# A two-layer kernel (attention with experts, then a state-space filter with a linear gate): the last attention group rearranged, output division moved later, third maximum scores moved ahead of a filler

## The chip, the cores and the metric

The kernel is one program on one NeuronCore of a Trainium2 chip. The metric is the device time of one execution in microseconds (us), lower is better; the figure shown is the median of three executions. PE is the matrix engine (TensorE), DVE the vector engine, ACT the scalar engine, POOL is GpSimd, SP the engine that only issues transfers here.

## What is computed

The input x is 4 sequences of 512 tokens with 512 values. Cut to what matters:

```python
xn = layernorm(x)
q, k, v = rope(xn @ wq), rope(xn @ wk), xn @ wv      # 32 heads of 16, 8 key/value heads
s = softmax(causal(q k^T / 4)) v @ wo
y = relu(xn @ W_e[top 2 of 8 experts] + b_e)          # mean of the two
x = x + s * silu(y.mean)
xn = layernorm(x)
K = s4_taps(Lambda, p, q, Vc, Ct, B, step)            # 512 real taps, by Cauchy sums and an inverse DFT
s = causal_convolution(xn, K) + D * xn
g = silu(xn @ dequant(weight).T + bias)
out = x + s * g
```

## The kernel before

The program has three parts, and each engine has its own list of instructions for each of them.

**Part a** (`sp_a`, `dve_a`, `pool_a`, `act_a`, `pe_a`) takes the 16 tiles of 128 tokens one after the other: layer norm, transposition, the products with wq, wk, wv and the gate, each value split in a high and a low part, rotation, and the ranking of experts. At its end the tokens are sorted into 39 expert tiles. While the vector engine makes the sorting tables, PE runs dummy products (`keep_awake`, L948), then `pe_back`, which needs those tables.

**Part b** (`dve_b`, `act_b`, `pool_b`, `sp_b`, `pe_b`) runs over 4 sequences b and 8 key/value heads h: 32 groups (b, h). A group of four query heads has ten *maximum scores* (`scores_1`, n = 0 to 9, L1563), whose row maxima DVE takes straight from the PSUM bank (`maxima`, L1374; three banks in turn, so scores n wait for maxima n - 3). DVE then writes the negated maxima as two parts (`maxima_parts`, L1387 and L1389), PE turns them (`turn_maxima`, L1600), DVE copies them (`maxima_rows`, L1397), and SP and ACT store them behind the group's queries (`maximum_rows`, L1291, semaphore b_mr). Ten *second scores* (`scores_2`, L1589 and L1592), the first of which waits for b_mr, contain the maximum; ACT takes exp (L1486), POOL clears the masked halves of four diagonal blocks (`select`, L1308), and PE multiplies with the values (`values`, L1616) into bank 4. DVE turns that bank (`rows_of`, L1407), divides by the row sums (`normalise`, L1412 and L1416) and, after every second group, turns the pair (`pair_rows`, L1424) for the output projection.

Three groups are in flight on PE: while second scores of (b, h) run, so do maximum scores of the next group, and 0 and 1 of the group after. Between them stand *fillers* (`quarters`, gaps 0 to 4): quarters of an expert tile (L1642, L1644) or of an output projection (`project`, L1655), six or eight in most groups, one or two in gap 4. DVE also turns gathered expert rows (`expert_x`, L1438) and makes the Cauchy sums of the filter in six steps for each of four pieces, one step in a group (`dve_s4`, L652 on); after the last piece it computes 512 complex roots in one go (L703 to L737), in group (3, 6). The inverse DFT (`pe_taps`, L762) is eight full-width products with broadcast weights in group (3, 7); the taps go to DRAM and come back as a Toeplitz tile (`sp_taps`).

**Part c** (`*_c`) is the second layer on 16 tiles: gather of expert outputs (`rows`, `more_rows` on POOL), gate, layer norm, then on PE a turn (L2061), the linear product (L2072) and the convolution (L2077). Before its first tile stand the last sequence's output projection (16 products, `project` in `pe_c`) and the scaling and splitting of the linear weights on DVE (`dve_scale`, L1878, L1884, L1887). `prepared(u)` on DVE (L1895 to L1917) makes the gated sum and statistics of tile u; `inverse_root` on POOL (L1850) needs them, and `shift`, the norm on ACT (L2026) and PE's turn follow.

The order of part b on PE, in the body of the loop over groups:

```python
scores(e, (2, 3, 4), following, (0, 1, 2), (b, h))
quarters(b, h, 0)
...
scores(e, (0, 1), after, (8, 9), (b, h))
quarters(b, h, 3)
for j in ORDER[1:]:
    values(e, b, h, j)
quarters(b, h, 4)
```

## Time and profile before

| | |
|---|---|
| median of 3 executions | 697.06 us (695.39 to 698.77) |
| the profiled execution | 695.48 us |
| its span, first to last instruction | 693.3 us |
| busy: PE, DVE, POOL, ACT | 92%, 80%, 51%, 42% |
| granted PE clock, mean | 0.97 |
| stretches: part a, part b, part c from its first linear product | 0 to about 104 us, to about 593 us, 607 us to the end |

The profiled execution is 2.2 us longer than its span and 1.6 us under the median. In a timeline row the first number is the start from the span's begin, the second the duration; what stands in brackets is the time its engine stood idle before it and what ended that. A group of rows by line gives busy time, mean duration in ns, and the idle time before. PE "busy" is modelled from the issue of its products. A granted clock of 1.00 is 2.4 GHz, 0.50 is 1.2 GHz.

### The profile page before, as it was taken

The numbers are of one execution on the slowest core, as the hardware profiler recorded it, in microseconds if no ns is written. First come the engines' busy times: TensorE is split into PE (matmuls) and PEld (weight loads), VectorE is DVE, ScalarE is ACT, GpSimd is POOL, SyncE is SP. The second block draws the span as 40 slices with busy tenths as digits, with TensorE's granted clock in tenths as the row PEclk, the third lists the DMA queues.
The fourth block names the chain that finished last, engine by engine and source line by source line (L and its number), as shares of the span: only waits on it lengthen the run. The fifth ranks groups of instructions, "written<-read, shape, count | busy, mean of one in ns | idle before, by whom it ended". The sixth has DMA issues, their size and how long they took to land.

```text
span 693.3 us, 12356 instructions
## 1 busy us (share of the span) xinstructions
PE 638.2 (92%) x3560; PEld 344.0 (50%) x3560; DVE 553.4 (80%) x1789; ACT 289.0 (42%) x535; POOL 351.1 (51%) x497
## 2 busy tenths in 40 slices
PE   8999997888989999989999898999998999999997
PEld 4888774433333334333443333443333443488886
DVE  5698898669987777987777798787887887769995
ACT  4353326234443444434454443444344543445441
POOL 3777531636764723466473245646415434566630
PEclk9999999569999999999999999999999999999999
DMA  7599989246667454272653606457063526758851
GB/s 251 151 330 281 331 195 180 50 68 179 106 191 125 98 96 75 40 134 77 114 96 64 92 22 131 106 99 128 20 117 64 142 80 215 152 119 220 201 132 76
DMA packets 55567, 92.67 MB, mean 134 GB/s; under 512 B 10328, under 2 KB 23320, under 8 KB 55504
## 3 DMA queue, kind: packets, MB, share of 16 engines
q1 hardware_dynamic: 41890, 66.45, 41.0%
q0 software_dynamic: 8576, 18.62, 12.7%
q10 hardware_dynamic: 5038, 6.84, 3.9%
q8 instruction: 29, 0.48, 0.3%
q14 instruction: 34, 0.28, 0.2%
HBM read 61.93 MB, written 29.43 MB: 132 GB/s over the span
## 4 chain that ended last, share of the span: by engine, by line
PE 46%; DVE 39%; issue 6%; DMA 3%; POOL 3%; SPq 1%; ACT 1%; ACTq 0%; DVEq 0%; POOLq 0%
DVE bank L1374 19%; PE bank L1644 10%; PE bank L1616 7%; PE bank L1563 6%; PE bank L2072 6%; DVE arena L1374 4%; PE bank L2077 4%; PE bank L991 4%; DMA turned_parts<-qk_parts 3%; DVE arena L1407 2%; PE bank L1655 2%; DVE m_parts L1387 2%; PE bank L1589 2%; PE bank L1600 2%; DVE arena L1424 2%
## 5 line engine op out<-in xcount | busy, mean ns | idle before, releaser
L1374 DVE CUSTOM_DVE_ANT_0 bank<-bank,cst 128x384 f32<-128x384 f32 (+3 forms) x512 | 234.0, 522 | 66.8 <-PE bank L1563 65.2
L1486 ACT ACTIVATE arena<-bank 128x512 f32<-128x512 f32 x320 | 172.7, 600 | 209.6 <-PE bank L1589 149.9
L1321 POOL DMA_INDIRECT arena<-xn_rows,slots_i x156 | 150.1, 962 | 55.0 <-issue 37.3
L1308 POOL TENSOR_SCALAR_AFFINE_SELECT arena<-arena 128x512 f32<-128x512 f32 x128 | 81.0, 647 | 182.9 <-ACT arena L1486 181.8
L1644 PE MATMUL bank<-w_e,arena 128*128 x312 | 160.4, 620 | 0.0
L1563 PE MATMUL bank<-kt,qt 48*128 48x512 f32 (+1 forms) x496 | 119.5, 352 | 15.3 <-DVE arena L1374 12.4
L1563 PEld LDWEIGHTS bank<-kt,qt 48*128 48x128 f32 x496 | 73.6, 193 | 101.6 <-DVE arena L1374 56.3
L1589 PE MATMUL bank<-qt,kt 50*128 50x512 f32 x256 | 92.2, 464 | 0.6 <-ACT arena L1486 0.6
L1616 PE MATMUL bank<-arena 128*32 128x512 f32 (+3 forms) x1024 | 88.0, 455 | 2.7 <-ACT arena L1486 2.3
L1644 PEld LDWEIGHTS bank<-w_e,arena 128*128 128x128 f32 x312 | 53.7, 192 | 57.5 <-issue 54.2
L1374 DVE DVE_READ_ACCUMULATOR2_ANT arena<- 128x1 f32 x512 | 72.0, 141 | 0.0
L1655 PE MATMUL bank<-w_proj,arena 128*128 128x512 f32 x128 | 66.9, 638 | 0.0
L991 PE MATMUL bank<-proj_high,xh 128*128 128x264 f32 (+1 forms) x128 | 45.9, 359 | 0.7 <-DVE xl L522 0.7
L825 POOL TENSOR_TENSOR s_tok<-arena 128x256 f32<-128x256 f32 (+1 forms) x64 | 33.4, 554 | 25.4 <-DVE arena L541 20.0
L1589 PEld LDWEIGHTS bank<-qt,kt 50*128 50x128 f32 x256 | 43.3, 191 | 4.3 <-ACT arena L1486 2.2
L1496 ACT ACTIVATE arena<-bank 128x512 f32<-128x512 f32 x39 | 23.4, 599 | 50.3 <-PE bank L1644 44.7
L1616 PEld LDWEIGHTS bank<-arena 128*32 128x32 f32 x1024 | 24.6, 110 | 39.3 <-issue 24.4
L991 PE MATMUL bank<-proj_low,xh 128*128 128x264 f32 (+1 forms) x128 | 43.5, 340 | 0.0
L991 PE MATMUL bank<-proj_high,xl 128*128 128x264 f32 (+1 forms) x128 | 43.2, 338 | 0.0
L1655 PEld LDWEIGHTS bank<-w_proj,arena 128*128 128x128 f32 x128 | 21.6, 193 | 27.4 <-issue 24.7
L1438 DVE STREAM_TRANSPOSE arena<-arena 128x512 f32<-128x512 f32 x39 | 27.5, 706 | 8.1 <-PE bank L1644 7.5
L537 DVE TENSOR_TENSOR arena<-bank,cst 128x128 f32<-128x128 f32 (+1 forms) x63 | 27.2, 475 | 5.9 <-PE bank L991 5.8
(168 smaller groups left out, 954.3 us busy)
## 6 DMA issues: line engine op xcount, KB each, us to landing
qt<-turned_parts SPq DMA_DIRECT2D x96, 128.0 KB
turned_parts<-qk_parts SPq DMA_DIRECT2D x8, 1280.0 KB
expert_rows<-arena SPq DMA_DIRECT2D x39, 256.0 KB
w_e<-in_L_ffn_W_e ACTq DMA_DIRECT2D x24, 256.0 KB, 6.1
kt<-turned_parts SPq DMA_DIRECT2D x96, 64.0 KB, 5.5
arena<-in_L_attn_x SPq DMA_DIRECT2D x16, 256.0 KB, 5.8
xn_rows<-arena SPq DMA_DIRECT2D x16, 256.0 KB, 5.7
w_e<-in_L_attn_x SPq DMA_DIRECT2D x16, 256.0 KB
```

Of the source, the lines that this page charges most:

```text
L825: i = g.tensor_tensor(o[:, :, :, c, :], xc[:, :, :, c, :], xs[:, :, :, 1 - c, :], op)
L991: i = t.matmul(out[u % 2][:, 0:n], x[:, u % 2, k, :], w[part][:, k, :], start=(k == 0 and x is xh and part == 0), stop=(k == KB - 1 and pa ...
L1308: g.affine_select(out=diag, in_=diag, compare_op=ALU.is_ge, fill=0.0, base=0, pattern=[[0, 2], [0, HALF], [1, P]], channel_multiplier=-1). ...
L1321: e.indirect_dma_start(xg[m % 2][:, n * P:(n + 1) * P], None, xn_q, bass.IndirectOffsetOnAxis(ap=slots_i[:, n, m:m + 1], axis=0)).then_inc ...
L1374: i = v.tensor_tensor_reduce(out=part, in0=part, in1=const("mask")[:, S - w:], scale=1.0, scalar=LOWEST, op0=ALU.add, op1=ALU.max, accum_o ...
L1486: nc.scalar.activation(pt[:, s, first:second + 1:second - first].rearrange("p c r q -> p c (r q)"), s2_bank(b, h, n).rearrange("p (c x) -> ...
L1563: i = t.matmul(s1_bank(b, h, n)[:, at:at + w], stack[rows, x if r is None else r, q * P:w], kt[rows, h // 2 % 2, h % 2, 0:w], start=(x == ...
L1589: i = t.matmul(to, keys(j), queries[:, q:q + 2], start=True, stop=True)
L1616: i = nc.tensor.matmul(bank[4][VW * r:VW * (r + 1), j * P:], vb[:, j, h, :], pt[:, r // HALF, at:at + TPB - j, r % HALF, :], start=(j == O ...
L1644: i = t.matmul(bank[7], xgt[:, m % 2, k * P:(k + 1) * P], w_e[:, ex[m], k, :], start=False, stop=(k == KB - 1))
L1655: i = t.matmul(bank[to], ot[:, (b * PAIRS + k) % (PAIRS + 1), u, :], wo[:, k, :], start=(k == 0), stop=(k == KB - 1))
L2072: i = t.matmul(bank[2 + u % 2][:, :], x[:, u % 2, k, :], (w_high, w_low)[part][:, k, :], start=(k + n == 0), stop=(k + n == KB + 1))
```

## The change

Seven edits, in the order of the program:

1. Part a, start: the second token tile is loaded behind the second of four blocks of wq, whose semaphore is split in two; statistics of tile 1 come ahead of the splitting of wq on DVE; ACT normalises tile 1 ahead of the other weights; PE turns tile 2 behind the q products of tile 1.
2. `keep_awake(16)` becomes `keep_awake(28)`.
3. The Cauchy steps run without a gap between pieces, so that the last piece ends in (3, 1), and the roots are made in four steps in groups (3, 2) to (3, 5) (`dve_roots`).
4. In a group on PE, maximum scores 2 (of the group after) and second scores 0 (of the next) stand behind the values, in front of gap 4.
5. In a group on DVE, for h > 0, the division and the turn of the pair stand behind maxima 0 and 1 of the group after, no longer between maxima 4 and 5.
6. The last group has a list of its own (`last_group`): twelve of the sixteen projection products of the last sequence stand between its scores and values, in four banks; the inverse DFT is eight 32-wide products plus one that sums the four strips; DVE divides the last group before it scales the weights, and splits the weights (`dve_scaled_parts`) after the statistics of the first tile of part c, before those of the second.
7. POOL gathers rows of tiles 1 and 2 of part c after the last select, no longer between selects. The DFT table is loaded a group earlier at its end.

The core of the diff:

```diff
@@ sp_a, dve_a, act_a, pe_a @@
-                e.dma_start(wq[:, k, :], wq_d[k * P:(k + 1) * P]).then_inc(a_wq, 16)
-            e.dma_start(xin[:, 1, :], x_t[1]).then_inc(a_x[1], 16)
+                e.dma_start(wq[:, k, :], wq_d[k * P:(k + 1) * P]).then_inc(a_wq[k // 2], 16)
+                if k == 1:
+                    e.dma_start(xin[:, 1, :], x_t[1]).then_inc(a_x[1], 16)
...
-            keep_awake(16, bank[0])
+            keep_awake(28, bank[0])
...
@@ dve_s4 @@
-            if not (isinstance(b, int) and b == NB - 1):
-                h -= 2
+            at = b * NG + h - 2
+            if at < 0:
+                return
+            piece, h = divmod(at, 6)
+            if piece == NB:
+                dve_roots(e, st, h)
...
+        def dve_tap_parts(e):
+
+            e.wait_ge(s4_parts, 1)
+            nc.vector.tensor_copy(tap_parts, bank[5]).then_inc(s4_taken, 1)
...
@@ pe_taps @@
-                e.wait_ge(b_m, NB * NG * NJ)
-            for k in range(KB):
-                i = t.matmul(bank[5], roots[:, c, k:k + 1].to_broadcast([P, P]), dft[c][:, k, :],
-                             start=(c + k == 0), stop=(c + k == KB))
+                for part in range(2):
+                    for k in range(KB):
+                        i = t.matmul(bank[5][32 * k:32 * (k + 1), :], roots[:, part, k:k + 1].to_broadcast([P, 32]), dft[part][:, k, :],
+                                     start=(part == 0), stop=(part == 1), skip_group_check=True)
+                i.then_inc(s4_parts, 1)
             if c == 1:
-                i.then_inc(s4_taps, 1)
+                e.wait_ge(s4_taken, 1)
+                t.matmul(bank[5], const("sel")[:, 0:1].to_broadcast([P, P]), tap_parts, start=True, stop=True).then_inc(s4_taps, 1)
...
@@ dve_b @@
-                    finish(*next_group(b, h, -1))
+                    done, later = next_group(b, h, -1), h > 0 and following
+                    rows_of(*done)
+                    if not later:
+                        divided(*done)
...
+                    if later:
+                        divided(*done)
                     if (b, h) == (NB - 1, NG - 1):
+                        dve_tap_parts(e)
+                        dve_taps(e, st)
+                        finish(b, h)
                         dve_scale(e)
-                        dve_taps(e, st)
                     dve_s4(e, st, b, h)
-                    if following is None:
-                        finish(b, h)
...
@@ pe_b @@
-                    scores(e, (2, 3, 4), following, (0, 1, 2), (b, h))
+                    scores(e, (3, 4), following, (1, 2), (b, h))
...
+                    scores(e, (2,), after, (0,), following)
                     quarters(b, h, 4)
+
+            def last_group(b, h):
...
+                e.wait_ge(b_m, NB * NG * NJ)
+                fill(0, 2)
+                scores(e, (), None, (1, 2), (b, h))
+                fill(2, 3)
+                scores(e, (), None, (3, 4), (b, h))
+                pe_taps(e, 0)
+                scores(e, (), None, (5, 6, 7), (b, h))
+                values(e, b, h, ORDER[0])
+                fill(3, 4)
+                scores(e, (), None, (8, 9), (b, h))
+                pe_taps(e, 1)
+                fill(4, 5)
+                values(e, b, h, ORDER[1])
+                fill(5, 6)
+                values(e, b, h, ORDER[2])
+                fill(6, 7)
+                values(e, b, h, ORDER[3])
+                fill(7, 12)
...
@@ dve_c @@
             e.wait_ge(b_s, TPB)
-            for u in range(2):
-                prepared(u)
+            prepared(0)
+            dve_scaled_parts(e)
             shift(0, 0)
+            prepared(1)
...
@@ pe_c @@
             for u in range(TPB):
-                if u > 1:
-                    e.wait_ge(b_s, (NB - 1) * TPB + u - 1)
-                if u == TPB - 1:
-                    turn(0, 0)
-                for k in range(KB):
-                    project(NB - 1, u, k, 7 - u % 2)
+                project(NB - 1, u, KB - 1, PROJECT_BANK[u])
+            e.wait_ge(b_s, (NB - 1) * TPB + 2)
+            turn(0, 0)
```

What moves, first on PE in group (3, 4) to (3, 5). L1616 (L1658 in the changed file) are values, L1563 (L1605) maximum scores, L1589 (L1631) second scores, L1644 (L1686) a filler. Before:

```order
L1616 MATMUL bank4<-arena 32x256 x4
L1616 MATMUL bank4<-arena 32x128 x4
L1616 MATMUL bank4<-arena 32x384 x4
L1644 ISA
L1644 MATMUL bank67<-w_e,arena 128x512
L1563 MATMUL bank5<-kt,qt_56 128x512
L1589 MATMUL bank67<-qt_56,kt 128x512
L1563 MATMUL bank0<-kt,qt_56 128x512
L1589 MATMUL bank2<-qt_56,kt 128x512
```

And in the changed kernel:

```order
L1658 MATMUL bank4<-arena 32x256 x4
L1658 MATMUL bank4<-arena 32x128 x4
L1658 MATMUL bank4<-arena 32x384 x4
L1605 MATMUL bank5<-kt,qt_56 128x512
L1631 MATMUL bank67<-qt_56,kt 128x512
L1686 ISA
L1686 MATMUL bank67<-w_e,arena 128x512
L1605 MATMUL bank0<-kt,qt_56 128x512
L1631 MATMUL bank2<-qt_56,kt 128x512
```

The pair of scores stands a filler earlier; nothing else changes places there.

DVE at the entry of part c: bank 4 is turned and divided for the last group (L1407 to L1424, in the changed file L1440 to L1457), the linear weights are scaled and split (L1878 to L1887; L1953 to L1966), and `prepared(0)` begins with a product into s_tok (L1895; L1974). Before:

```order
L1878 TENSOR_TENSOR w_e<-w_e,arena 128x512 x4
L1884 CAST w_high_60<-w_e 128x512 x4
L1887 TENSOR_TENSOR w_low_61<-w_e,w_high_60 128x512 x4
L744 MEMSET arena 128x128
L745 COPY arena<-bank5 128x512
L747 TENSOR_TENSOR arena<-arena,d_c 128x1
L1407 STREAM_TRANSPOSE arena<-bank4 128x512
L1412 RECIPROCAL arena<-arena 128x16
L1416 TENSOR_TENSOR arena<-arena 128x16x16
L1424 STREAM_TRANSPOSE arena<-arena 128x512
L1895 TENSOR_TENSOR s_tok<-s_tok,w_e 128x512
```

And in the changed kernel:

```order
L1440 STREAM_TRANSPOSE arena<-bank4 128x512
L1445 RECIPROCAL arena<-arena 128x16
L1449 TENSOR_TENSOR arena<-arena 128x16x16
L1457 STREAM_TRANSPOSE arena<-arena 128x512
L1953 TENSOR_TENSOR w_e<-w_e,arena 128x512 x4
L1974 TENSOR_TENSOR s_tok<-s_tok,w_e 128x512
L1980 TENSOR_TENSOR s_tok<-s_tok,w_e 128x512
L1985 BN_STATS arena<-s_tok 128x6
L1991 BN_AGGR arena<-arena 128x2
L1996 TENSOR_SCALAR arena<-arena 128x1
L1963 CAST w_high_60<-w_e 128x512 x4
L1966 TENSOR_TENSOR w_low_61<-w_e,w_high_60 128x512 x4
```

The weight work that stood ahead of the last division now stands behind it, and its split behind the first `prepared`.

## Rows read from the trace of the kernel before

**Rows 1.** The stretch of the groups, 150 to 573 us, busy us of PE, PEld, DVE, ACT, POOL.

```profile
150.00:573.00 423.00, 389.73 (x2206) 162.63 (x2204) 339.27 (x1251) 180.57 (x338) 214.60 (x265) 0.99 0.51 100
```

**Rows 2.** The same stretch: who waited, for whom (us in total, times, longest).

```profile
PE bank L1600 <- DVE m_parts L1389: 12.8, 24, 1.0
...
DVE bank L1374 <- PE bank L1563: 59.6, 34, 5.3
```

**Rows 3.** The same stretch, PE groups by form (busy, mean ns, idle before).

```profile
L1563 PE MATMUL bank<-kt,qt 48*128 48x256 f32 x116 | 26.8, 323 | 12.9 <-DVE arena L1374 10.1 <-issue 2.7
```

**Rows 4.** PE timeline, one period (start us, us, what).

```profile
501.33 0.28 PE L1600 MATMUL bank<-cst,m_parts 128*32 128x128 f32 x1 [0.86 <-DVE m_parts L1389]
...
504.69 1.98 PE L1644 MATMUL bank<-w_e,arena 128*128 x4
...
515.87 0.28 PE L1600 MATMUL bank<-cst,m_parts 128*32 128x128 f32 x1 [0.27 <-DVE m_parts L1389]
```

**Rows 5.** DVE timeline, the same period.

```profile
507.24 0.70 DVE L1374 CUSTOM_DVE_ANT_0 bank<-bank,cst 128x512 f32<-128x512 f32 x1 [1.95 <-PE bank L1563]
...
510.02 0.25 DVE L1412 RECIPROCAL arena<-arena 128x16 f32<-128x16 f32 x1
510.31 0.42 DVE L1416 TENSOR_TENSOR arena<-arena 128x256 f32<-128x256 f32 x1
510.76 0.71 DVE L1424 STREAM_TRANSPOSE arena<-arena 128x512 f32<-128x512 f32 x1
```

**Rows 6.** The store of turned maxima: ACT queue timeline, then PE weight loads.

```profile
501.96 0.62 ACTq L1291 DMA_DIRECT2D qt<-arena  x1
...
573.81 0.62 ACTq L1291 DMA_DIRECT2D qt<-arena  x1
...
576.45 0.29 PEld L1589 LDWEIGHTS bank<-qt,kt 50*128 50x128 f32 x3 [0.62 <-DMA qt<-arena]
```

**Rows 7.** PE timeline around the dummy products, then 116 to 148 us (us, busy, clock, DMA).

```profile
108.56 3.63 PE L948 MATMUL bank<-ones_b 128*128 128x512 bf16 x16
115.25 1.97 PE L1156 MATMUL bank<-arena 128*128 128x78 bf16 x32 [3.06 <-DVE arena L1089]
...
116.00:148.00 32.00, 25.92 (x159) 0.55 0.31 55
```

**Rows 8.** PE groups by form, last group and projections, 573 to 607 us.

```profile
L1655 PE MATMUL bank<-w_proj,arena 128*128 128x512 f32 x32 | 14.2, 595 | 0.0
L762 PE MATMUL bank<-v_tok,roots 128*128 128x512 f32 x8 | 5.4, 840 | 0.4 <-DVEq L737 0.4
L762 PE MATMUL bank<-s_tok,roots 128*128 128x512 f32 x8 | 3.7, 605 | 0.0
...
L1616 PE MATMUL bank<-arena 128*32 128x512 f32 x8 | 1.1, 604 | 0.0
```

**Rows 9.** DVE groups, 584 to 595 us, then its timeline.

```profile
L1887 DVE TENSOR_TENSOR w_low<-w_e,w_high 128x512 fp32r<-128x512 f32 x4 | 2.5, 684 | 0.0
L1878 DVE TENSOR_TENSOR w_e<-w_e,arena 128x512 f32<-128x512 f32 x4 | 2.5, 686 | 2.9 <-DMA arena<-n_L_ffn_weight_scale_inv 2.9
L1884 DVE CAST w_high<-w_e 128x512 fp32r<-128x512 f32 x4 | 2.3, 634 | 0.0
...
592.54 0.72 DVE L1407 STREAM_TRANSPOSE arena<-bank 128x512 f32<-128x512 f32 x1
...
594.68 0.65 DVE L1895 TENSOR_TENSOR s_tok<-s_tok,w_e 128x512 f32<-128x512 f32 x1
...
597.31 0.68 DVE L1895 TENSOR_TENSOR s_tok<-s_tok,w_e 128x512 f32<-128x512 f32 x1
```

**Rows 10.** Entry of the second layer: POOL timeline, then PE timeline.

```profile
608.26 0.57 POOL L1850 TENSOR_TENSOR arena<-arena,cst 128x1 f32<-128x1 f32 x1 [3.57 <-DVE arena L1917]
...
618.27 0.66 PE L2061 MATMUL bank<-cst,w_e 128*128 128x128 f32 x4 [1.25 <-ACT w_e L2026]
```

**Rows 11.** PE timeline at the start of the program.

```profile
22.57 0.66 PE L961 MATMUL bank<-cst,arena 128*128 128x128 f32 x4 [0.96 <-ACT arena L858]
```

More of the change, by code:

```diff
@@ L975, in sequence @@
                         e.wait_ge(a_xl[u % 2], nth(b, u))
-                    if (u + 1 < TPB or more) and (b, u) != (0, 0):
+                    early = b == 0 and u < 2
+                    if (u + 1 < TPB or more) and not early:
                         turn(b + (u + 1) // TPB, (u + 1) % TPB)
@@ L2042, in act_c @@
             gate(e, 0, 2)
-            projected(e, NB - 1, 3, 6)
             gate(e, 0, 3)
```

135 lines of the change are left out of this document (81 added, 54 removed).

## The prediction

> **What bounds the kernel now.** I read the busy time by stretch first. The groups fill 423 us of the 693, and PE is busy for 389.7 of them, DVE for 339.3 [rows 1]: PE is the bound, with 33 us of gaps, and the reader should ask who makes the gaps. The waits answer: PE stood 12.8 us in 24 places before the turn of the maxima, for DVE [rows 2], and 12.9 us before the last maximum scores (n = 8 and 9), nearly all for DVE too [rows 3]. Together that is 25.7 us, and it is odd, for DVE itself stood 59.6 us waiting for PE's maximum scores [rows 2]. So neither is full; they wait for each other in turn. The timelines of one period show how. PE turned maxima at 501.33, 0.86 late; its values ended at 504.69, and then came two products of filler in front of the third maximum scores [rows 4]. DVE had run dry 1.95 us before it could start on those scores at 507.24; later, between its fifth and sixth maxima, it spent 510.02 to 511.47 on the division and the turn of the pair [rows 5], at a time when PE was about to ask for maxima, and the next turn of maxima came 0.27 late [rows 4].
>
> **The steady groups.** The edit on PE puts the third scores at about 504.7 instead of 506.6, so DVE can take them up to 1.9 us sooner; the edit on DVE moves 1.45 us (in every second group the 0.25 and 0.42 alone, 0.7) to before them, into the time in which it stood idle [rows 5]. In this period, then, the sixth maxima begin when their scores are there, 1.7 us earlier than before, and the turn, late by 0.27, would have over a microsecond in hand. The arithmetic of PE does not change, so the gain can be no more than its waits for DVE: 25.7 us [rows 2, 3]. Not all of it comes back. Three times in the program `expert_x` on DVE stands behind the expert of gap 4, so that DVE still starts late; the Cauchy steps and expert turns fill most of the idle time into which the division goes; and where maxima end just behind a select on POOL DVE's small operations are long already. I take 70%, 18 us. From below I bound it at 9 (about a third: the waits before scores 8 and 9 go by two thirds, those at the turn stay), from above at 25.7.
>
> What the moved pair of scores is late for next is a transfer. Second scores 0 wait for the store of the turned maxima. That store is issued 0.63 us behind the turn (501.96 against 501.33) and in the one place where PE came early, at 573.81, its landing was over by 576.45, 2.64 us later [rows 6]; that makes 3.27 behind the turn. In the new order PE wants it 3.4 to 3.6 us behind the turn (504.69 - 501.33 = 3.36, and the product of third scores) [rows 4]. I cost this at nothing, covered by 0.1 to 0.3 us; without the cover each 0.1 us costs 3 us over 30 groups.
>
> The Trainium skill, "DMA: Bandwidth & Descriptors", section "Issuing engines are not separate DMA queues", says that transfers of all issuing engines run on the same 16 DMA engines and interleave, so that issuing on ACT and SP buys no private path. By that rule the store lands later when stacks and gathers are in flight. The trace neither confirms nor denies it for this store: PE never came early enough elsewhere.
>
> **Start of the program.** The loads and statistics of tile 1 move ahead, and DVE's statistics of tile 2, on which POOL's memsets and the norm of tile 3 hang, come some 0.7 us sooner (one statistics pass no longer stands in between). PE waited 0.96 us for that norm and is then full [rows 11]. Between 0 and -0.9; part of it is lost where part a later waits for transfers, so -0.4.
>
> **Dummy products.** Sixteen took 3.63 us, twelve more take 2.7 and fill most of the 3.06 us in which PE waited [rows 7]: they end about 0.3 us before the tables are there. What they buy is the clock: behind that wait its mean from 116 to 148 us was 0.55, nearly all at the 1.2 GHz level [rows 7]. About 3 us of products at full clock instead of half give 1.2 us (half of the 1.97 us of `pe_back` and a little behind it). Bounds: +0.3 if they end late, -8 if the clock then stays up until 148 us (PE is busy for 25.92 us there, about half of which a full clock would save, and I let a third of that be covered by waits for others), which I doubt, since PE stands idle again, 6 of the 32 us, and the half clock outlasted those 25.92 us of products [rows 7]. The Trainium skill, "TensorE: Matmul & The Clock Gate", Part 1, has idleness bring the half clock back; by it the later pause undoes the gain behind it, and the term is the 1.2 us taken here.
>
> **The last group and the entry of the second layer.** Let T be the last turn of maxima, 573.81 - 0.63 = 573.18 [rows 6]. The last values ended at 592.5, T + 19.3, where DVE turns bank 4 [rows 9]. Out of PE's way go 5.4 + 3.7 us of inverse DFT and some 1.3 us of waits; in come two sets of narrow products, each like the values' four at 1.1, one full product of 0.9, and seven projections of 14.2 / 16 = 0.89 each [rows 8]: T + 19.3 - 9.1 - 1.3 + 3.1 + 6.2 = T + 18.2. PE then has nine projections left, 8.0 us, done at T + 26.2, where before it was done at T + 33.5. This is where the gain would seem to be, and I count none of it, because DVE takes over. Behind the last values it has the division (0.72, 0.25, 0.42, 0.71: 2.1), the scaling (2.5), `prepared(0)` (597.31 - 594.68 = 2.6), the split of weights (2.3 + 2.5), `prepared(1)` (2.6), the Toeplitz split and the low part of tile 0 (three passes like the 0.68 of L1887, 2.0), then `prepared(2)` (2.6) [rows 5, 9]: 19.4, so POOL can take the root of tile 2 at T + 37.6. Before, the 7.3 us of scaling and splitting lay under PE's inverse DFT, and that root began at 608.26, T + 35.1 [rows 10]. What follows it up to the third tile's products is POOL's series of gathers and roots, unchanged, which made PE stand 1.25 us at 618.27 [rows 10]. So the entry is late by 2.5 us; as overlaps of a few tenths are likely I take +2. Bounds: +4 with the clock falling while PE waits for DVE from T + 26 on, -2 if DVE's series runs beside the gathers better than one after another. The roots, for which PE waited 0.4 us [rows 8], move to groups (3, 2) to (3, 5), under PE's work, at most eight operations in each; the cover is the idle time of DVE, and without it they cost, at no more than the 0.25 us of the small reciprocal [rows 5], up to 2 us in each. From the second tile on part c is unchanged.
>
> **The sum.** -0.4 - 1.2 - 18 + 2 = -17.6, from 695.48 us of the profiled execution: 677.9. The median of the runs is 1.6 above that execution, which gives 679.5; I say 679.
>
> **Rivals.**
> *Half the gain.* DVE is the next bound: the work that a group needs from it is 339.3 / 29 = 11.7 us (the 116 products of rows 3, four a period, make 29 periods) against PE's 389.7 / 29 = 13.4, and the heavy groups lie above that mean. Then 9 us come back: 688. For it: the selects on POOL that lengthen its small operations, and that every idle microsecond into which the division goes may be wanted. Against: in the period of rows 5 it fits. 0.17.
> *The clock stays up after the dummy products*, and the early groups run at full clock: 8 us instead of 1.2, 672. Against it the pauses behind them. 0.09.
> *Nothing comes of it:* the waits for DVE turn into waits for ACT to empty bank 7 and for exps, as PE arrives earlier at both: 695. The change moves only order, so this can be. 0.07.
> *Slower, by the store of the maxima.* The store lands behind the second scores' turn and each group stalls PE, the bound. Its place is the first second scores, its price 30 times (landing after issue - 2.97 us), and it cancels the 18 us when the landing takes 3.6 us. At 3.8 us it costs 25: 677.9 + 25 + 1.6 = 704. For it: that the measured case, 2.64, was a quiet moment, and the rule above. Against: it may take over a third longer before it decides. 0.05.
>
> **How the numbers follow.** The forecast's own case, 672 to 685, has 0.62. The range goes from 670, which takes in most of the clock case and of the upper bound of the group term, to 691, which takes in the half gain and its upper errors; it leaves out the last two rivals and the tails. About 0.5% (3.5 us) is what a measurement of this kernel can tell from no change. Faster: 0.62 + 0.17 + 0.09 = 0.88, less 0.01 for a half gain that turns out smaller, 0.87. Same: 0.07 and that 0.01, 0.08. Slower: 0.05.
>
> **What would show it.** Right: PE's waits before the turn of maxima and before scores 8 and 9 fall from 25.7 to under 9 us, DVE's wait for maximum scores shrinks, periods shorten from 423 / 29 = 14.6 to about 14.0 us, no wait of PE's weight loads for the store, a clock above 0.55 behind the dummy products, and 2 us more than before between the last turn of maxima and the third tile's products of the second layer. Wrong: a long total of waits for the store, periods of 14.6 us with waits under another name, or PE in the second layer starting earlier than T + 33 after the last turn.

## The result and the profile after

The changed kernel takes 691.48 us (median of 13 executions, 687.97 to 693.93), the kernel before 695.05 beside it: ratio 0.9933, interval 0.9911 to 0.9955. That is 0.7% faster where 2.5% was forecast; the direction held, the size did not, and 691.5 lies just outside the range. A second measurement on a chip like this one gave 0.9945 (0.9923 to 0.9968). Some experiments ran on chips on which the kernel before takes 683 us; there the changed kernel came to 0.9966 (0.9937 to 0.9995). So every ratio below is to the kernel before on the same chip. "First kind" is a chip of 695 to 698 us, "second kind" one of 683; several chips of each were used, and only runs that are said to be of one set were measured side by side. Executions in a slower state (up to 974 us) are left out of the ratios.

The profiled execution took 689.92 us, its span is 688.0. The stretch of the groups, who waited for whom (columns: us in total, times, longest), to be read against [rows 2]:

```profile
PE bank L1642 <- DVE m_parts L1422: 10.8, 19, 1.7
PE bank L1658 <- ACT arena L1528: 8.0, 7, 1.5
PE bank L1684 <- ACT arena L1538: 3.6, 3, 1.7
PE bank L1605 <- DVE arena L1407: 2.7, 8, 0.5
...
DVE bank L1407 <- PE bank L1605: 28.3, 42, 3.2
...
DVE bank L1407 <- remote: 15.7, 10, 2.4
```

DVE's wait for maximum scores fell from 59.6 to 28.3, or to 44.0 with the 15.7 for which the profile names no releaser ("remote"), and PE's wait for DVE before maximum scores fell from 10.1 [rows 3] to 2.7. But the wait at the turn of maxima nearly stayed, 12.8 to 10.8, and one grew that was 1.9 us before: values wait 8.0 us for ACT (4.4 in a second profile of the changed kernel, 2.0 in a second one of the kernel before).

The ledger by marks on PE, in us: end of part a (first turn of maxima) at 102.17 before, 102.42 after; from there to the next turn 29.8 and 27.7; from that to the last turn 441.2 and 433.8; behind it to the end 120.2 and 124.1. So +0.2, -2.1, -7.5, +3.9, in sum -5.4 before rounding. Forecast were -0.4, -1.2, -18 and +2. In the third stretch PE stood idle for 36.2 us before and 30.8 after, so only 5.4 us of the 7.5 are idle time that went; the other 2.1 are a balance of the clock, of the cut run and of what a wait costs beyond its idle time, each treated below.

**Why the turn still waits.** DVE, then POOL, then PE in one period after:

```profile
518.15 0.15 DVE L1407 DVE_READ_ACCUMULATOR2_ANT arena<- 128x1 f32 x1
518.33 1.40 DVE L1420 TENSOR_SCALAR m_parts<-arena 128x16 fp32r<-128x16 f32 x1
519.76 0.18 DVE L1422 SCALAR_TENSOR_TENSOR m_parts<-arena,m_parts 128x16 fp32r<-128x16 f32 x1
```

```profile
517.49 0.95 POOL L1357 DMA_INDIRECT arena<-xn_rows,slots_i  x1 [0.17 <-issue]
518.45 1.24 POOL L1344 TENSOR_SCALAR_AFFINE_SELECT arena<-arena 128x512 f32<-128x512 f32 x2
```

```profile
519.99 0.28 PE L1642 MATMUL bank<-cst,m_parts 128*32 128x128 f32 x1 [1.35 <-DVE m_parts L1422]
```

An operation on 128x16 numbers, 0.17 us elsewhere, takes 1.40 and ends at 519.73, just when POOL's two selects end (519.69). The wait is booked on DVE; POOL held it. This is not new: in the whole profile 13 first and 7 second parts took over 0.5 us, before 11 and 8, and both parts together 22 us against 24. DVE's earlier start did not take them out of the selects' way. The Trainium skill, "SBUF — State Buffer", section "Who interferes with whom", says that DVE and GpSimd share one port pair and that the later of two instructions that want it is blocked for the whole of the other. In all 20 cases a select runs beside the long part, and in 18 it is recorded as starting first, so the trace agrees; in the row shown DVE starts 0.12 us before the selects, while POOL still issues a gather.

**Why the values wait.** PE, DVE, ACT's queue and ACT, then PE again, in another period after:

```profile
548.05 0.28 PE L1642 MATMUL bank<-cst,m_parts 128*32 128x128 f32 x1
...
551.93 0.85 PE L1658 MATMUL bank<-arena 128*32 128x384 f32 x8 [1.09 <-ACT arena L1528]
```

```profile
549.76 0.28 DVE L1430 COPY arena<-bank 32x128 f32<-32x128 f32 x1 [1.14 <-PE bank L1642]
```

```profile
550.07 0.62 ACTq L1327 DMA_DIRECT2D qt<-arena  x1
550.79 1.09 ACT L1528 ACTIVATE arena<-bank 128x512 f32<-128x512 f32 x2 [3.38 <-PE bank L1658]
```

The copy of the turned maxima comes 1.71 us behind the turn (0.32 to 0.50 in most groups); ACT's store stands behind it, and the last two exps behind the store. They end at 551.88, and the values start at 551.93. From 150 us on ten groups have a copy over 0.9 us behind the turn, two in the profile before.

**What the moved pair costs PE.** From the end of the values to the filler of gap 0, PE before and after, the same work:

```profile
517.81 1.50 PE L1616 MATMUL bank<-arena 128*32 128x256 f32 x24
519.24 1.12 PE L1655 MATMUL bank<-w_proj,arena 128*128 128x512 f32 x2
520.30 0.50 PE L1563 MATMUL bank<-kt,qt 48*128 48x512 f32 x1
...
521.20 1.99 PE L1655 MATMUL bank<-w_proj,arena 128*128 128x512 f32 x4
```

```profile
508.22 1.50 PE L1658 MATMUL bank<-arena 128*32 128x256 f32 x24
509.65 0.49 PE L1605 MATMUL bank<-kt,qt 48*128 48x512 f32 x1
509.65 0.50 PE L1631 MATMUL bank<-qt,kt 50*128 50x512 f32 x1
510.08 1.13 PE L1697 MATMUL bank<-w_proj,arena 128*128 128x512 f32 x2
511.14 0.49 PE L1605 MATMUL bank<-kt,qt 48*128 48x512 f32 x1
...
511.81 1.98 PE L1697 MATMUL bank<-w_proj,arena 128*128 128x512 f32 x4
```

Without a wait in either, 519.24 to 521.20 is 1.96 us and 509.65 to 511.81 is 2.16. The other groups without a wait there say the same: 1.95 to 1.97 and 2.15 or 2.16 (once 2.23) with one quarter of filler in gap 4, 2.82 and 3.10 with two, 2.94 and 3.14 with two and the bias product that begins an expert tile. For the 15, 7 and 7 groups of these sorts that makes some 6.4 us, an estimate from these rows. With the waits, which fell a little, the stretch takes 74.6 us before and 79.7 after in 29 groups, 0.18 more a group. The six products are the same run cut in two, and cutting it costs.

**The clock** had a part as well. The stretches around one wait of PE before, and the same place after (us, busy of PE, PEld, DVE, ACT, POOL, clock, DMA):

```profile
366.00:367.00 1.00, 0.69 (x6) 0.49 (x8) 1.00 (x5) 0.37 (x1) 0.00 (x0) 1.00 0.93 109
...
368.00:371.50 3.50, 3.50 (x11) 1.11 (x7) 1.89 (x10) 0.00 (x0) 1.23 (x2) 0.54 0.21 81
```

```profile
364.00:368.00 4.00, 3.99 (x34) 1.71 (x35) 3.20 (x9) 1.09 (x2) 0.00 (x0) 1.00 0.03 8
```

Before, PE stood 1.26 and 0.26 us in front of scores 8 and 9 there, and then ran 3.5 us at the 1.2 GHz level; so again at 484 us. After it stood 0.39 and 0.26 and the clock stayed at 2.4 GHz. The two periods around the first dip took 16.07 and 14.55 us, eight groups earlier 15.70 and 13.91; those around the second 16.22 and 14.07. So a dip costs 0.7 to 1.0 us, and the two some 1.7 of the 7.5 us by which the groups got shorter in these two profiles. In other profiles of versions like the changed one, dips stand elsewhere (none to three), so this is no sure gain.

**The entry of part c.** DVE, POOL and PE behind the last turn, T = 563.86:

```profile
582.26 0.72 DVE L1440 STREAM_TRANSPOSE arena<-bank 128x512 f32<-128x512 f32 x1 [3.75 <-PE bank L1658]
...
586.77 0.69 DVE L1974 TENSOR_TENSOR s_tok<-s_tok,w_e 128x512 f32<-128x512 f32 x1
...
593.30 0.69 DVE L1974 TENSOR_TENSOR s_tok<-s_tok,w_e 128x512 f32<-128x512 f32 x1
```

```profile
602.48 0.59 POOL L1922 TENSOR_TENSOR arena<-arena,cst 128x1 f32<-128x1 f32 x1
...
610.66 1.15 POOL L1922 TENSOR_TENSOR arena<-arena,cst 128x1 f32<-128x1 f32 x1
```

```profile
594.38 0.63 PE L2141 MATMUL bank<-cst,w_e 128*128 128x128 f32 x4 [4.27 <-ACT w_e L2106]
598.18 1.09 PE L2141 MATMUL bank<-cst,w_e 128*128 128x128 f32 x4 [3.18 <-ACT w_e L2106]
...
612.91 0.66 PE L2141 MATMUL bank<-cst,w_e 128*128 128x128 f32 x4 [2.46 <-ACT w_e L2106]
```

Bank 4 is turned at T + 18.4, the root of tile 2 comes at T + 38.6 (T + 35.1 before, [rows 10]), the fourth tile's turn at T + 49.0 (before 618.27 - 573.18 = 45.1). PE, done with the projections at T + 26, idles 10 us in three places instead of 1.25. Its clock fell too, to a mean of 0.51 from 595 to 602 us, where before it was 1.00 at this place; but PE waited 2.46 us for the fourth tile's norm behind that, so the lateness there is not the clock's.

### The profile page after: what moved, and what is told of

It reads as the page before. It is cut to its first block, busy times and chain, and to the rows that moved or that the text cites. A ratio compares the mean times of both kernels' runs of the same rounds, so it can differ in the third digit from the quotient of the medians.

```text
span 688.0 us, 12390 instructions
## 1 busy us (share of the span) xinstructions
PE 631.9 (92%) x3574; PEld 338.7 (49%) x3574; DVE 551.4 (80%) x1790; ACT 290.2 (42%) x535; POOL 354.2 (51%) x497
## 3 DMA queue, kind: packets, MB, share of 16 engines
q0 software_dynamic: 8576, 18.62, 12.7%
## 4 chain that ended last, share of the span: by engine, by line
PE 57%; DVE 24%; DMA 5%; issue 5%; POOL 3%; another core or an unknown queue 2%; ACT 1%; SPq 1%; ACTq 0%; DVEq 0%; POOLq 0%
PE bank L1686 14%; DVE bank L1407 11%; PE bank L1605 8%; PE bank L1658 7%; PE bank L1697 6%; PE bank L2152 6%; PE bank L2157 4%; PE bank L1024 4%; DMA turned_parts<-qk_parts 3%; PE bank L1631 3%; PE bank L1642 2%; DVE arena L1407 2%; DVE m_parts L1420 2%; PE bank L1684 1%
## 5 line engine op out<-in xcount | busy, mean ns | idle before, releaser
L1407 DVE CUSTOM_DVE_ANT_0 bank<-bank,cst 128x384 f32<-128x384 f32 (+3 forms) x512 | 235.2, 522 | 54.3 <-PE bank L1605 33.0
L1686 PE MATMUL bank<-w_e,arena 128*128 x312 | 160.7, 621 | 0.0
L1605 PE MATMUL bank<-kt,qt 48*128 48x512 f32 (+1 forms) x496 | 120.9, 350 | 4.4 <-DVE arena L1407 4.2
L1605 PEld LDWEIGHTS bank<-kt,qt 48*128 48x128 f32 x496 | 71.7, 191 | 101.9 <-DVE arena L1407 49.9
L1631 PE MATMUL bank<-qt,kt 50*128 50x512 f32 x256 | 97.6, 469 | 0.4 <-ACT arena L1528 0.4
L1658 PE MATMUL bank<-arena 128*32 128x512 f32 (+3 forms) x1024 | 88.3, 453 | 9.4 <-ACT arena L1528 8.0
L1686 PEld LDWEIGHTS bank<-w_e,arena 128*128 128x128 f32 x312 | 53.5, 191 | 51.2 <-issue 47.1
L1407 DVE DVE_READ_ACCUMULATOR2_ANT arena<- 128x1 f32 x512 | 73.1, 143 | 0.0
L1658 PEld LDWEIGHTS bank<-arena 128*32 128x32 f32 x1024 | 24.5, 110 | 48.6 <-issue 28.0
L1631 PEld LDWEIGHTS bank<-qt,kt 50*128 50x128 f32 x256 | 42.5, 187 | 5.2 <-ACT arena L1528 3.3
```

Of the source, the lines that this page charges most:

```text
L1407: i = v.tensor_tensor_reduce(out=part, in0=part, in1=const("mask")[:, S - w:], scale=1.0, scalar=LOWEST, op0=ALU.add, op1=ALU.max, accum_o ...
L1605: i = t.matmul(s1_bank(b, h, n)[:, at:at + w], stack[rows, x if r is None else r, q * P:w], kt[rows, h // 2 % 2, h % 2, 0:w], start=(x == ...
L1631: i = t.matmul(to, keys(j), queries[:, q:q + 2], start=True, stop=True)
L1658: i = nc.tensor.matmul(bank[4][VW * r:VW * (r + 1), j * P:], vb[:, j, h, :], pt[:, r // HALF, at:at + TPB - j, r % HALF, :], start=(j == O ...
L1686: i = t.matmul(bank[7], xgt[:, m % 2, k * P:(k + 1) * P], w_e[:, ex[m], k, :], start=False, stop=(k == KB - 1))
```

## The experiments

**The two edits of the groups, apart** (second kind, one set).

```diff
-                    scores(e, (3, 4), following, (1, 2), (b, h))
+                    scores(e, (2, 3, 4), following, (0, 1, 2), (b, h))
...
-                    scores(e, (2,), after, (0,), following)
```

> The changed kernel with its score pair back behind the filler of gap 4 (edit 4 undone); the division stays deferred. Theory A (the groups' gain of about 7.5 us came mostly from DVE starting on the third scores sooner; what is left of PE's waits is held by POOL, whose selects keep DVE's small operations back): 4 to 6 us longer than the changed kernel, and PE's waits before scores 8 and 9 back to 6 us or more of their 10. Theory B (the two edits are only worth something together): the whole 7 us come back. Theory C (the division alone did it): within 1.5 us of the changed kernel.

Measured: 674.62 us, ratio 0.988 (0.9859 to 0.9901). Undoing the edit made the kernel faster than any measurement of the changed one, which none of the theories had.

```diff
-                    done, later = next_group(b, h, -1), h > 0 and following
+                    done, later = next_group(b, h, -1), False
```

> The changed kernel with the division back between the fifth and sixth maxima (edit 5 undone); the score pair stays moved. Theory A: 1.5 to 3.5 us longer than the changed kernel, since the 0.7 or 1.4 us lie again before the turn of maxima, but DVE starts 1.9 us sooner. Theory B: 7 us longer. Theory C: 5 us or more longer. In all of them PE's wait at the turn of maxima rises.

Measured: 684.14 us, 1.0019 (0.9996 to 1.0041). With both undone:

> Both edits of the groups undone, the rest of the changed kernel kept. All theories: 7 to 8 us longer than the changed kernel, the gain between the second and the last turn of maxima in the two profiles. Were it under 4, the groups got shorter by something else (the Cauchy steps' new places, the clock). The entry of the second layer, which took 3.9 us more behind the last turn than before, should stay as it is.

Measured: 685.48 us, 1.0049 (1.003 to 1.0068). PE's waits of this one by the count of the section above: 14.1 at the turn, 13.5 before scores 8 and 9. The deferred division is worth 1.0049 - 0.988 = 1.7%. Without it the moved pair gains 0.3%, with intervals that overlap, and the other edits together cost 0.5%.

To know what the pair does beside the deferral, the changed kernel was measured twice more, the second time on a chip of the second kind:

> The changed kernel, unedited, beside the kernel before on the chip of these runs. The first four experiments were measured on a chip on which the kernel before takes 683.1 us, not 695, and leaving the score pair where it was gave a ratio of 0.988 there. Theory F (moving the score pair costs 3 to 4 us once the division is deferred): ratio 0.991 to 0.996 again. Theory G (the two chips differ in what the change is worth, and the pair costs nothing): ratio 0.985 to 0.99.

Measured on the first kind: 0.9945 (0.9923 to 0.9968).

> The changed kernel, unedited, as the measure for the three experiments beside it: ratio 0.991 to 0.997 to the kernel before if this is a chip on which that one takes 695 us. On one where it takes 683, this is the missing term: 0.991 to 0.996 by theory F (the moved score pair costs, since 0.988 was measured without it), 0.985 to 0.99 by theory G (the chips differ).

Measured on the second kind: 680.51 us, 0.9966 (0.9937 to 0.9995). Against 0.988 without the pair's move, in another set, that is 0.9%, 5.9 us. The expectation F is right in direction and was too small there. The kernel of the first experiment, unedited, on the first kind:

> The first experiment again (score pair behind the filler, division deferred), beside the others of this call. Theory F' (each time PE goes from a filler to two scores and back it loses 0.18 us, read off the start times: the pair and its filler take 2.15 us apart and 1.97 together, 31 times 0.18 = 5.6 us, less what DVE gains by its earlier start): ratio 0.986 to 0.991 whatever the chip. If the first result was a lucky one: 0.993 to 0.997 like the changed kernel.

Measured: 0.9916 (0.989 to 0.9941), just above what F' allowed: 0.2 to 0.3% better than the changed kernel, which was measured in other sets, not 0.9. These intervals overlap, so this run alone does not show a cost. By the medians the pair costs 6 us on the second kind and about 2 on the first, each time across sets. The start times do not differ between the kinds: without a wait 1.96 us with the pair back and 2.15 with it moved on the second too, 2.81 and 3.10 with two quarters of filler.

**What holds the turn.** POOL's selects cut to 16 elements, two times eight, with the pattern to match (most of the masking of the diagonal blocks is left out):

```diff
-                diag = pt[:, :, BLOCKS.index((j, j))]
+                diag = pt[:, :, BLOCKS.index((j, j)), 0, 0:8]
```

> The changed kernel with each of POOL's selects cut to 2 x 8 elements of the 512: most of the masking of the diagonal blocks is left out. Count, order and semaphores stay. Theory A (POOL's instructions keep DVE's first maxima part and its copy of the turned maxima back, and by the copy ACT's store and the exps behind it): PE's waits at the turn of maxima fall from 10.8 to under 4 us, those of the values for ACT from 8.0 to under 4, the time falls by 7 to 12 us. Theory D (DVE's own amount of work is the next bound): under 2 us. Theory E (the exps are late by themselves, since second scores come late): the turn waits fall, those of the values stay, 3 to 6 us.

Measured: 670.69 us, 0.9824 (0.9804 to 0.9845) on the second kind, 9.8 us under the changed kernel on that kind. PE's turn, and DVE's first part:

```profile
L1642 PE MATMUL bank<-cst,m_parts 128*32 128x128 f32 x29 | 8.2, 282 | 1.9 <-DVE m_parts L1422 0.7
L1420 DVE TENSOR_SCALAR m_parts<-arena 128x16 fp32r<-128x16 f32 x29 | 5.7, 195 | 1.0
```

In the changed kernel on that kind these were

```profile
L1642 PE MATMUL bank<-cst,m_parts 128*32 128x128 f32 x29 | 8.2, 283 | 9.6 <-DVE m_parts L1422 9.4
L1420 DVE TENSOR_SCALAR m_parts<-arena 128x16 fp32r<-128x16 f32 x29 | 10.5, 362 | 1.0
```

The wait of 9.4 us at the turn (from 150 to 555 us) becomes 0.7 when POOL is out of the way. DVE has the same operations; the first parts take 4.8 us less, the second ones 4.2 (9.6 to 5.4), together about what the turn no longer waits. Theory A holds for the turn, D falls. The other half of A is not tested here: on this kind the values waited only 4.1 us for ACT in the changed kernel, now 3.0.

Whether the form of the instruction matters:

```diff
-            v.tensor_scalar(m_parts[:, :, 0], rows, -1.0, None, ALU.mult)...
+            v.scalar_tensor_tensor(out=m_parts[:, :, 0], in0=rows, scalar=-2.0, in1=rows, op0=ALU.mult, op1=ALU.add)...
```

> The changed kernel with the first part of the negated maxima computed from two reads of the maxima (-2 m + m, the same value) by the instruction that makes the second part, not by the one-input form. The one-input form took 1.2 to 1.4 us beside two selects on POOL and ended with them; the two-input form takes at most 0.6 beside them. Theory A (the form is what is held back): its mean falls from 0.44 to under 0.3 us, PE's waits at the turn from 10 to 6 or 7, the time by 2 to 4 us. Theory H (any DVE instruction that reads SBUF is held as long): no change.

Measured: 0.9948 (0.9922 to 0.9974) against 0.9966 in the same set, no difference; the mean of the instruction was 0.465 us against 0.362, not under 0.3. Both forms are held: H.

**What makes the copy late.** The copy on ACT, on the first kind:

```diff
-            nc.vector.tensor_copy(m_rows, S1_BANK[...]...)
+            (copy or nc.vector.tensor_copy)(m_rows, S1_BANK[...]...)
...
+                        maxima_rows(e, *next_group(b, h, 1), nc.scalar.copy)
                         maximum_rows(e, *next_group(b, h, 1), 1)
```

> The changed kernel with the copy of the turned maxima taken from DVE and given to ACT, right before ACT's own store of them. In the changed kernel's profile that copy came 1.3 to 2.1 us behind the turn in ten groups (0.3 to 0.5 in the others), and the store and the last two exps stand behind it. Theory A (POOL's selects and gathers, and the expert turn in front of it on DVE, keep the copy back): PE's waits of the values for ACT fall from 8.0 to under 3 us and the time by 4 to 8 us. Theory B' (the copy is late because PE's turn ends late, whoever reads it): no more than 1 us, or 0.2 us a group slower for ACT's slower copy.

Measured: 0.9918 (0.989 to 0.9946) against 0.9945 in the same set, 2 us, within the intervals. ACT's copy and PE's turn in one group:

```profile
462.65 0.28 PE L1641 MATMUL bank<-cst,m_parts 128*32 128x128 f32 x1
```

```profile
464.32 0.25 ACT L1430 COPY arena<-bank 32x128 f32<-32x128 f32 x1 [1.68 <-PE bank L1641]
```

ACT had been idle and its copy is 1.67 us behind the turn, as DVE's was in this group of the changed kernel (1.70). So neither DVE's queue nor its port makes the lateness in such a group: B', and my theory A fell for this half. The values' wait for ACT was 3.7 us and the turn's 13.1; in the changed kernel of the same set they were 4.4 and 9.5. So the 8.0 us of the first profile are not what this edit would save.

Both edits at once, the copy on ACT and the pair's move undone:

> As the experiment with the score pair back behind the filler, and the copy of the turned maxima on ACT. There DVE's copy came up to 3.5 us late behind a turn of expert rows that waited for its gather. If that is a cost of its own, this one is 2 to 5 us faster than that experiment (ratio to the kernel before 0.981 to 0.985); if not, within 1 us of its 0.988.

Measured: 686.31 us, 0.9866 (0.9845 to 0.9886), in the same set as the 0.9918, with intervals that do not overlap: the pair's move costs 0.5%, 3 us by the medians. This is the one comparison side by side with the division deferred.

The traces of the two pairs of one set say why the move gains 0.3% in one and loses 0.5% in the other. From the third turn of maxima to the last, PE's time outside its recorded waits grew by 6.4 us with the move when the division was not deferred (383.1 to 389.5, the kernel with both edits undone and the one with the division back), and by 5.1 when it was (388.6 to 393.7, the two with the copy on ACT). Its recorded waits fell by 7.9 us in the first pair (32.4 to 24.5) and by only 4.4 in the second (30.7 to 26.3). The cost of the cut is there in both; what DVE's earlier start gives back is smaller once the deferral has been made.

**Dummy products** (second kind), as many as before:

```diff
-            keep_awake(28, bank[0])
+            keep_awake(16, bank[0])
```

> The changed kernel with sixteen dummy products again, not twenty-eight. Between the turn at the end of part a and the next one it should take longer again by what the dummy products bought: 1.2 us by my prediction's term, 2.1 us by the two profiles (29.8 against 27.7 us); so 1 to 2.5 us slower than the changed kernel. If a part of those 2.1 came from the moved start, under 1.

Measured: 680.78 us, 0.9954 against 0.9966 in the same set: nothing lost. From the end of part a to the next turn it took 29.5 us against 28.5, but to the turn after that 40.5 against 40.4. The clock with 28 products (the changed kernel of the same set) and here (16):

```profile
116.00:125.00 9.00, 7.02 (x76) 4.72 (x76) 6.91 (x24) 5.59 (x12) 2.12 (x4) 0.76 1.09 138
125.00:150.00 25.00, 22.26 (x107) 9.28 (x101) 16.84 (x65) 6.18 (x11) 14.01 (x16) 0.54 0.30 57
```

```profile
116.00:125.00 9.00, 7.23 (x92) 5.40 (x91) 6.78 (x24) 4.52 (x9) 1.29 (x2) 0.73 1.08 149
125.00:150.00 25.00, 21.29 (x112) 9.12 (x110) 18.13 (x68) 8.14 (x15) 14.50 (x17) 0.62 0.26 53
```

With 28 products the clock was hardly higher in the first stretch (0.76 against 0.73) and lower in the second (0.54 against 0.62). What was gained at once, `pe_back` in 1.51 us instead of 1.94, is gone by then.

**The entry of part c.** POOL's gathers back between the selects (second kind):

```diff
                     select(b, h, 0)
+                    if (b, h) == (NB - 1, NG - 1):
+                        rows(e, 0, 0)
...
+                        for u in (1, 2):
+                            rows(e, 0, u)
                     select(b, h, 3)
```

> The changed kernel with the gathers of tiles 0 to 2 of part c back between the selects of the last group on POOL (edit 7 undone), in the order of the kernel before. In the changed kernel the first gather comes 12.2 us behind the last turn of maxima, before 6.5; everything on POOL behind it is late, and PE waits 2.46 us for the norm of the fourth tile. Theory P (POOL's gathers set the entry): 1.5 to 3 us faster, the fourth tile's turn at 46 to 47.5 us behind the last turn instead of 49.0. Theory Q (DVE's scaling, division and first statistics set it, as I predicted): within 0.7 us.

Measured: 0.9931 (0.9903 to 0.9958) against 0.9966 in the same set, intervals overlapping; behind the last turn 123.6 us instead of 124.2, the fourth tile's turn at T + 48.5. By the profile Q.

```diff
+                        dve_scale(e)
+                        dve_scaled_parts(e, True)
                         finish(b, h)
-                        dve_scale(e)
...
-            dve_scaled_parts(e)
+            dve_scaled_parts(e, False)
```

> The changed kernel with the scaling of the linear weights and their high parts ahead of the last group's division on DVE, in the 3.8 us in which DVE stands idle there; the low parts stay behind the first tile's statistics. Theory Q (DVE's queue behind the last values sets the entry of part c: 22.9 us to the first tile's sum, 38.6 to the third tile's root, as the prediction had it): the third tile's root comes 2.5 to 4 us sooner and the stretch behind the last turn falls from 124.1 to between 120 and 122 us. If the gathers set it (theory P), under 1 us.

Measured: 0.9947 (0.9922 to 0.9972) on the first kind, 124.2 us behind the last turn: nothing. The chain moved, though. DVE is ready at 585.3 and stands:

```profile
587.51 0.69 DVE L1975 TENSOR_TENSOR s_tok<-s_tok,w_e 128x512 f32<-128x512 f32 x1 [2.25 <-ACT w_e L1857]
```

ACT waited for gathered rows, until 586.78. So DVE's queue and POOL's gathers are about equally late, and each hides the other; neither Q alone nor P alone accounts for both runs.

```diff
                 for u in range(TPB):
+                    if TPB * b + u + 3 < NT:
+                        inverse_root(b + (u + 3) // TPB, (u + 3) % TPB)
                     if TPB * b + u + 6 < NT:
                         rows(e, b + (u + 6) // TPB, (u + 6) % TPB)
...
-                    if TPB * b + u + 3 < NT:
-                        inverse_root(b + (u + 3) // TPB, (u + 3) % TPB)
```

> The changed kernel with POOL's root of a tile in front of the two gathers of its turn in part c, not behind them. In its profiles the root of the fourth tile comes 8.2 us behind that of the third, in a queue of four gathers, though DVE's statistics are there some 3 us earlier. Theory P2 (the entry is DVE's lateness plus this queue): PE's wait for the fourth tile's norm (1.4 to 2.5 us) goes and the stretch from the last turn of maxima to the end falls from 124.1 to 121.5 to 122.7 us. Theory R (what bounds the entry is when gathers land, so later tiles wait instead): under 0.7 us.

Measured: 706.34 us, 1.0142 (1.0108 to 1.0177), 136.9 us behind the last turn: 12.7 more. Neither theory had a loss. POOL in one tile:

```profile
618.89 0.57 POOL L1922 TENSOR_TENSOR arena<-arena,cst 128x1 f32<-128x1 f32 x1 [3.65 <-DVE arena L1996]
```

With the root first, POOL's wait for DVE stands in front of the gathers, the gathers land later, DVE's next statistics wait for them, and so round: from 565 us on ACT waits 41.0 us for gathered rows and POOL 33.0 for statistics, in the changed kernel 16.8 and 19.1.

The pair's move undone and the three edits of part c together (gathers back, scaling ahead, roots first):

> An attempt at the best: the changed kernel with the score pair behind the filler (0.988 in the experiment), the gathers back between the selects (0.5 us behind the last turn), POOL's roots first and the scaling ahead. If the four add up: ratio 0.979 to 0.984, the stretch behind the last turn 118.5 to 120.5 us.

Measured: 1.0115 (1.0078 to 1.0152), 136.6 us behind the last turn, the same fault; the fourth tile's turn came at T + 47.9, 1.1 us sooner than in the changed kernel. Roots first alone had it at T + 48.9, so most of that is the other two edits.

**Pieces put together** (first kind). The pair's move undone, the copy on ACT, gathers back and scaling ahead:

> The changed kernel with the score pair behind the filler, the copy of the turned maxima on ACT, the gathers back between the selects and the scaling ahead of the last division; roots not first. The first two gave 0.9866 together; the last two gave nothing one at a time, but DVE waited for gathers in the one and POOL for DVE in the other, so together they should bring the stretch behind the last turn from 124.2 to 121.5 to 123 us. Ratio 0.982 to 0.987.

Measured: 685.86 us, 0.9845 (0.9815 to 0.9875), and 123.2 us behind the last turn, at the slow end of what was expected there (121.5 to 123). It beats the kernel before by 1.5% and, across sets, the changed one by about 0.9%. The last one edits the kernel before, by the deferred division alone:

```diff
+                    done, later = next_group(b, h, -1), h > 0 and following
+                    rows_of(*done)
+                    if not later:
+                        divided(*done)
...
+                    if later:
+                        divided(*done)
```

> The kernel before with the deferred division alone. Theory F' (the deferral is the part that gains, 1.7% between the two experiments with the pair back; the other edits together cost 0.5%, mostly the 4 us behind the last turn): ratio 0.982 to 0.987, and 120 us behind the last turn. If the gain needs the other edits (roots out of the way, the start): 0.99 or more.

Measured: 688.92 us, 0.9875 (0.9849 to 0.9901), just above F'. One edit of seven gives more than all seven (0.9933 and 0.9945 on this kind, in other sets). PE in the groups and at the last group of this kernel:

```profile
PE bank L1625 <- ACT arena L1495: 9.2, 7, 1.8
PE bank L1609 <- DVE m_parts L1389: 7.9, 16, 0.8
...
PE bank L1572 <- DVE arena L1374: 3.1, 6, 0.8
```

```profile
573.42 5.75 PE L762 MATMUL bank<-v_tok,roots 128*128 128x512 f32 x8 [2.58 <-DVEq L737]
```

The waits before scores 8 and 9 are 3.1, without any move on PE. They had a price beyond their idle time. From the first of the eight products of scores 8 and 9 to the values behind them PE takes 1.20 us where it waited, of which 0.26 is a second recorded wait, and 0.68 where it did not; so each such place costs 0.26 us more than the profile books as waiting. From 150 us on there are 15 such places before and 3 here (3 in the changed kernel too). That is a part of why the groups got shorter though PE's recorded waits did not: from the third turn to the last they are 33.5 us before and 36.1 here, the time outside them 393.8 and 384.4. Twelve places fewer make 3.1 of these 9.4 us, one dip of the clock less about 1; the rest is not accounted for.

The roots, made at one go, are now late by 2.58 us (0.44 before), which is 2.1 of the 3 us by which it takes 123.2 behind the last turn and not 120. That dividing the roots, edit 3, would take this wait away was not run on this kernel; in the changed one, which divides them, PE does not stand there.

A run of the unedited kernel before for its profile (697.17 us) gave the same waits as [rows 2, 3]: 12.8 at the turn, 10.6 before scores 8 and 9 put down to DVE, and half-clock dips at the same two places.

## Why the prediction was right and wrong

- **That PE's waits bound the groups, made by DVE's order**: right before scores 8 and 9, where the deferral alone took 7 of the 10.1 us put down to DVE; at the turn POOL's selects made most of them.
- **"The arithmetic of PE does not change, so the gain can be no more than its waits"**: this step failed. The products are the same and their time is not: the cut run of scores costs 0.2 to 0.3 us a group, 5.1 and 6.4 us in the two pairs of one set. The recorded waits were no measure from the other side either: a place with a wait before scores 8 and 9 also costs 0.26 us that is not booked as waiting. I moved the pair to let DVE start earlier and had priced only DVE's side. Beside the deferred division the move came out as a loss, 0.5% in the one set that had both, 0.2 to 0.9% across sets.
- **70% of 25.7, 18 us**: this term was mis-sized. Measured 7.5, some 1.7 of it from two dips of the clock that were not in the forecast. The waits before scores 8 and 9 went as forecast; those at the turn, 12.8, went to 10.8 and not to a third. I had named POOL's selects as a reason for a discount, from the long small operations, but not seen that a select sets the end of the parts whatever DVE does before them: 8.7 of 9.4 us of PE's waits in the experiment. The rival of half the gain, 688, was the nearest and had its reason there; DVE as the bound by its amount of work, which I gave for it, was refuted: with short selects DVE has the same operations and the kernel is 9.8 us faster.
- **A grown wait**, values for ACT, 8.0 us in one profile of the changed kernel and 4.4 in another, was in no term of the sum. I had listed the places, in another case ("waits for ACT to empty bank 7 and for exps" in the rival of no change).
- **Dummy products, -1.2**: the two profiles show -2.1 to the next turn; side by side it was -1.0, and gone by the turn after. Size zero.
- **Start, -0.4**: the third tile's turn came at 21.88 us instead of 22.57 [rows 11], as forecast, though PE waited 1.84 us for that norm instead of 0.96, and part a ended at 102.42 instead of 102.17. In the profiles of this study it ended between 100.0 and 103.7 whatever the version, so no effect of the start can be told.
- **Entry of part c, +2**: measured +3.9, about my upper bound. The steps held (bank 4 at T + 18.4 for 18.2, third tile's root at T + 38.6 for 37.6; the steps as written add up to 19.2, not 19.4, and the turn that I called the third tile's is the fourth one), the allowance for overlap did not exist, and the gathers, which I took as unchanged, were as late as DVE.
- **The store of the maxima**: PE never waited for it. That rival fell.
- **The chance**: 0.87 for faster was borne out, but one edit of seven alone gives more than the whole; the likeliest case took the ceiling of waits as the base and left no room for a cost of the move itself.

## What to carry to other kernels

Price a moved instruction on its own engine too: compare start-to-start times of the same products in one run and in pieces, and with and without a wait in them. When a small operation is late, look at what the neighbour engine does when it ends; if both end together, making it start earlier gains nothing. And test a bundle of edits one by one: here one of them carried the gain and one was a loss beside it.

## What was not expected

The stretch of six score products and a filler costs 0.20 us more when the run is cut (0.28 or 0.29 with two quarters of filler, 0.20 where the bias product stands in it), alike on both kinds of chip; no row shows why.

The turned maxima are read 0.9 to 2.4 us behind PE's turn, with the reader (DVE or ACT) standing idle until then, in six to eleven groups in the profiles of versions with the deferral on the first kind, and in two in those of the kernel before. On the second kind there is no such group: its one to four late copies all stand behind an expert turn on DVE that waited for its gather. In the profile of the changed kernel PE stood under 0.2 us before the turn in these groups, in other profiles up to 1.3. Either the recorded start of the turn is earlier than its work, or its signal is late; this stays open, as does the 1.8% between the kinds of chip, of which it may be a part.

Nearly thirteen microseconds were lost by putting one short operation ahead of two transfers in POOL's queue.
